# Attention 0 of a two-layer block: smoothing scales loaded ahead of the second half of the context, and tokens rounded in another order of operations

## The reference, cut to what matters

```python
def _div_clamp_fp8(x, scale):
    y = jnp.clip(x.astype(jnp.float32) / scale, -FP8_MAX, FP8_MAX)
    y = y.astype(jnp.bfloat16).astype(jnp.float32)
    return _fp8_roundtrip(y)

def _fp8_linear_pertensor(x, wq, w_scale, in_scale):
    xq = _div_clamp_fp8(x, in_scale)
    return jnp.einsum('bsi,oi->bso', xq * in_scale, wq) * w_scale
...
ln_out = _ln(hidden_states, ln_w, ln_b)
q = _fp8_linear_pertensor(ln_out, wq, wq_scale, q_in_scale).reshape(b, s, g, hpg, d)
...
catq = _div_clamp_fp8(cat, proj_smooth)
return jnp.einsum('bsi,oi->bso', catq, wproj) * (proj_in_scale * proj_w_scale)
```

## Time and profile before

| | before |
|---|---|
| median of 3 runs | 1565.88 us |
| lowest and highest | 1557.8 and 1568.2 us |
| the profiled execution | 1563.18 us, span 1561.4 us |
| PE, PE weight load busy | 88%, 76% |
| DVE busy | 78% |
| ACT, POOL busy | 65%, 50% |

### The profile page before, as it was taken

The page is one execution under the profiler, slowest core; times in us unless marked ns, Lnnn a source line. Parts: engine busy times, 40 slices in busy tenths (PEclk is TensorE's granted clock), DMA queues, the critical chain, the costliest instruction groups (busy, mean ns, idle before and its releaser), DMA issues. The chain is left out here.

```text
span 1561.4 us, 30287 instructions
## 1 busy us (share of the span) xinstructions
PE 1380.8 (88%) x11712; PEld 1183.6 (76%) x11712; DVE 1221.7 (78%) x2380; ACT 1013.3 (65%) x2152; POOL 782.9 (50%) x788
## 2 busy tenths in 40 slices
PE   0577999999999999999999996999779898894995
PEld 0466899999999999999999984677436565563995
DVE  6899888888888888898898897533359887876554
ACT  3687777877878778777777774312147565662773
POOL 4778566566666565666664453101123433331673
PEclk9889999999999999999999998999969998995997
DMA  3100010100100000001010002340350002003563
GB/s 102 47 15 28 15 22 15 32 5 15 35 15 16 22 14 17 20 15 35 15 31 22 1 1 90 70 59 21 66 163 2 14 2 68 1 14 134 186 213 128
DMA packets 62238, 69.84 MB, mean 45 GB/s; under 512 B 5424, under 2 KB 54800, under 8 KB 61968
## 3 DMA queue, kind: packets, MB, share of 16 engines
q1 hardware_dynamic: 59488, 60.54, 13.9%
q0 software_dynamic: 2432, 7.34, 1.4%
q10 hardware_dynamic: 176, 0.04, 0.0%
HBM read 55.56 MB, written 12.34 MB: 43 GB/s over the span
## 5 line engine op out<-in xcount | busy, mean ns | idle before, releaser
L880 POOL TENSOR_TENSOR RB<-YS,M 128x512 bf16<-128x512 f32 x128 | 161.6, 1263 | 245.3 <-DVE YS L740 245.3
L566 ACT ACTIVATE QT<-B,sm 128x256 f32<-128x256 f32 x256 | 130.8, 562 | 163.4 <-PE B L422 163.4
L442 PE MATMUL SS<-QT,KT 128*128 128x256 f32 x512 | 156.8, 401 | 10.0 <-DVE mx L695 10.0
L1748 POOL TENSOR_SCALAR_AFFINE_SELECT P<-P 128x1024 f32<-128x1024 f32 x64 | 82.3, 1285 | 154.3 <-ACT P L1602 154.3
L876 POOL TENSOR_TENSOR yy<-vv,half 128x12 f32<-128x12 f32 x64 | 147.4, 2303 | 5.3
L390 PE MATMUL PA<-WH,XQ 128*128 128x256 f32 x512 | 142.3, 309 | 6.3 <-ACT SQ L595 6.3
L392 PE MATMUL PA<-WL,XQ 128*128 128x256 f32 x512 | 130.5, 286 | 0.0
L714 DVE TENSOR_TENSOR QN<-QN,yy 128x512 f32<-128x512 f32 x128 | 125.0, 977 | 4.1 <-POOL yy L876 4.1
L707 DVE TENSOR_REDUCE vv<-SQ 128x6 f32<-128x768 f32 x128 | 120.6, 942 | 0.4 <-ACT SQ L598 0.4
L695 DVE TENSOR_REDUCE mx<-SS 128x4 bf16<-128x512 f32 x128 | 88.0, 688 | 40.5 <-PE SS L434 39.8
L410 PE MATMUL PA<-W,XB 128*128 128x128 bf16 x1536 | 109.5, 222 | 3.2 <-POOL XB L817 3.2
(11 more groups left out here) (328 smaller groups left out, 4489.8 us busy)
## 6 DMA issues: line engine op xcount, KB each, us to landing
W<-in_w SPq DMA_DIRECT2D x16, 1024.0 KB
Q<-qsc SPq DMA_DIRECT2D x48, 128.0 KB
WR<-in_wprojT SPq DMA_DIRECT2D x16, 256.0 KB, 3.0
K<-ksc SPq DMA_DIRECT2D x12, 256.0 KB
qsc<-T POOLq DMA_DIRECT2D x8, 384.0 KB, 4.2
X<-in_x SPq DMA_DIRECT2D x4, 512.0 KB, 5.7
CR<-in_xctxT SPq DMA_DIRECT2D x8, 256.0 KB, 2.9
RSM<-rsm_d SPq DMA_DIRECT2D x16, 128.0 KB, 4.2
```

What stands on the lines that cost most here:

```text
L442: pe.matmul(SS[:, 256 * z:256 * z + 256], k[:, 128 * z:128 * z + 128], q[:, 256 * z:256 * z + 256], start=True, stop=False)
L566: a.activation(QT[i % 2][:, o:o + 256], B1[:, o:o + 256], ACT.Identity, bias=col(n + "b"), scale=col(n + "w"))
L880: p.tensor_tensor(RB[i % 2][:], YS[:], M[:], ALU.subtract).then_inc(s_rb, 1)
```

## The change

- SP issues the store and the load of the smoothing scales right behind the weights of group 0, and the second half of the context after them.
- ACT scales y by -1/scale (a new tile scn) instead of by 2^20/scale. It no longer signals y by itself, and writes m of chunk i when DVE is done with chunk i-1's place, s_qs i-1, instead of waiting for POOL.
- DVE has two operations for a chunk instead of three: max(m, QMIN) + y into QS, then max(m, QMIN) - QS into QS. Neither y nor m is clamped above. The first of them waits for POOL's chunk i-2.
- POOL clamps QS between -448 and 448 with one tensor_scalar instead of subtracting m.
- DVE has one small operation more at the start, for scn.

```diff
@@ sp_attention_0
-            sp_context(sp, 1)
             sp.wait_ge(s_srv, 1)
             sp.dma_start(rsm_d.rearrange("a (c d) -> (a c) d", d=256), SRR).then_inc(s_sr, 16)
             sp_smooth(sp, 0)
+            sp_context(sp, 1)
@@ act_quad_scale
-            sc = scq[:, k, c:c + 1]
-            a.activation(QY[i % 3][:], LNT[:, c], ACT.Copy, scale=sc).then_inc(s_qy, 1)
+            a.activation(QY[i % 3][:], LNT[:, c], ACT.Copy, scale=scn[:, k, c:c + 1])
             if i >= 2:
-                a.wait_ge(s_q, i - 1)
-            a.activation(QM[i % 2][:], LNT[:, c], ACT.Abs, scale=sc).then_inc(s_qm, 1)
+                a.wait_ge(s_qs, i - 1)
+            a.activation(QM[i % 2][:], LNT[:, c], ACT.Abs, scale=scq[:, k, c:c + 1]).then_inc(s_qm, 1)
@@ dve_quad_round
-            v.wait_ge(s_qy, i + 1)
-            v.tensor_scalar(y[:], y[:], QMAX, -QMAX, ALU.min, ALU.max).then_inc(*vs.up())
             v.wait_ge(s_qm, i + 1)
-            v.tensor_scalar(m[:], m[:], QMIN, QMAX, ALU.max, ALU.min).then_inc(*vs.up())
-            v.wait_ge(*vs.at())
             if i >= 2:
                 v.wait_ge(s_q, i - 1)
-            v.scalar_tensor_tensor(out=s_[:], in0=y[:], scalar=1.0 / TWO20, in1=m[:], op0=ALU.mult, op1=ALU.add).then_inc(s_qs, 1)
+            v.scalar_tensor_tensor(out=s_[:], in0=m[:], scalar=QMIN, in1=y[:], op0=ALU.max, op1=ALU.add).then_inc(*vs.up())
+            v.wait_ge(*vs.at())
+            v.scalar_tensor_tensor(out=s_[:], in0=m[:], scalar=QMIN, in1=s_[:], op0=ALU.max, op1=ALU.subtract).then_inc(s_qs, 1)
@@ pool_quad_round
-            p.tensor_tensor(dst, QS[i % 2][:], QM[i % 2][:], ALU.subtract).then_inc(s_q, 1)
+            p.tensor_scalar(dst, QS[i % 2][:], 448.0, -448.0, ALU.min, ALU.max).then_inc(s_q, 1)
```

More of the change, by code:

```diff
@@ L200, in build @@
         scq = sb("scq", [128, 4, 2])
+        scn = sb("scn", [128, 4, 2])
         csc = sb("csc", [128, 4, 2])
@@ L251, in build @@
         s_zm, s_zroot, s_zv = (sem(n) for n in ("zm", "zroot", "zv"))
-        s_qturn, s_lnt, s_qy, s_qm, s_qs, s_q = (sem(n) for n in ("qturn", "lnt", "qy", "qm", "qs", "q"))
+        s_qturn, s_lnt, s_qm, s_qs, s_q = (sem(n) for n in ("qturn", "lnt", "qm", "qs", "q"))
         s_c, s_ch, s_ctx = (sem(n) for n in ("c", "ch", "ctx"))
@@ L754, in dve_attention_0 @@
             for k in range(4):
-                v.tensor_scalar(scq[:, k, :], scq[:, k, :], TWO20, None, ALU.mult)
-                t = v.tensor_scalar(csc[:, k, :], sm[:, AT[kinds[k]]:AT[kinds[k]] + 2], col(scales[k]), None, ALU.mult)
-            t.then_inc(s_sc, 1)
+                v.tensor_scalar(scn[:, k, :], scq[:, k, :], -1.0, None, ALU.mult).then_inc(*vs.up())
+                v.tensor_scalar(csc[:, k, :], sm[:, AT[kinds[k]]:AT[kinds[k]] + 2], col(scales[k]), None, ALU.mult)
+            v.wait_ge(*vs.at())
+            v.tensor_scalar(scq[:], scq[:], TWO20, None, ALU.mult).then_inc(s_sc, 1)
             v.wait_ge(s_sr, 16)
```

## The result

The changed kernel takes **1553.64 us** (median of 13 runs, 1546.66 to 1558.69) where the kernel before took 1564.48 on the same chip (median of 13, 1557.8 to 1576.11). The ratio is 0.9919, with a 95% interval of 0.9895 to 0.9942: faster by 0.8%. Of the ways that I had set down it is nearest to rival 2, the light clamp (1553 us), to which I had given 14%.

What follows compares the result with a forecast made beforehand. DVE's queue bounds the first 160 us, with a wait for the smoothing scales before the loop. Load -7.5, start +6.7 and loop +11.5 make +10.7 us on the profiled 1563.2, so 1574 us, range 1554 to 1589.

Steps and rivals of the forecast that it cites:

- rival 2: POOL's clamp in each chunk is light, 0.75 us: start -0.9, loop -1.3, together -9.7, 1553 us; chance 0.14.
- The earlier load: Before the loop: smoothing scales stored and loaded sooner, POOL's L838 starts at about 19.5 instead of 26.98, -7.5 us.
- p: Duration of POOL's clamp of 512 columns, L817 in each of 32 chunks, taken as 1.5 us.
- The bound below: Lower bound for POOL's 512-column clamp, from the one-input select L1748: about 0.7 us.
- The mutual exclusion: In the chunks, DVE and POOL shut each other out for whole instructions; whichever asked second waits for all of the other.
- the start: Replay from POOL's L843 to the third group of DVE's L179: +6.7 us with a clamp of 1.5 us.
- the loop: Chunks of quarters 1 to 3, iterations n = 1 to 11, on DVE's path: +11.5 us.
- My formula: Loop cost per iteration: 0.5 + (p - 1.15) for n = 1 to 5, 0.5 + 2 x (p - 1.15) for 6 to 11.
- The term for L732: From n = 6 on, DVE's L732 waits for POOL's second clamp, so p - 1.15 counts twice per iteration.
- the same replay: Start worked through operation by operation on DVE and POOL: +6.7 us with p = 1.5, -0.9 with p = 0.75.
- That ACT's lifted waits give nothing: In the loop, ACT no longer waiting for POOL gains nothing, since DVE was not waiting for ACT.

Runs made afterwards that it cites:

- rounding alone: Changed kernel with the smoothing scales' store and loads back in their old place, so only the new DVE and POOL chunk operations: 1559.34 us, ratio 0.9966 against before.
- the fastest kernel: Changed kernel with DVE's four operations per pair of chunks reordered and POOL's weight scaling L829 as a two-tile tensor_tensor with broadcast scale: 1543.04 us, ratio 0.9852 against before.
- the removed one back: Changed kernel with a third DVE operation per chunk, clamping y in place between -448 and 448 ahead of the other two: 1559.26 us, ratio 0.9942 against before.
- reordered pair: Changed kernel with the adding operations of both chunks of a pair first on DVE, then both subtracting ones: 1547.87 us, ratio 0.9894 against before.
- the series on POOL: Changed kernel with POOL operations of several forms and widths appended behind its last POOL work, in two runs, to price them; kernel time says nothing.
- the first series: Changed kernel with clamp, multiplications and subtraction appended on POOL at 128, 256 and 512 columns; at 512 the clamp took 0.63 us, multiplication by a tile's scale 1.65.

## Why the prediction was wrong

**The earlier load was right**: -7.5 forecast, L838 at 19.38 where I said 19.5, and 7.4 us passed on whole to the last chunk. It landed by the queue as worked out; the store took until 14.17 where I had 13.5.

**The step that failed is p.** The sum took 1.5 us for POOL's clamp of 512 columns, from the line through L829's rows at 128 and 256 columns; it measured 0.61. The bound below was wrong too: 0.7, from the select. I had reasoned that the same instruction in the trace is the nearest row. It was nearest by name; by form (one operation with a scale, against two with constants) it was another price, 1.65 against 0.63. The row of the select, one input and far away by name, gave the value within 0.1. The Trainium skill, "GPSIMD Engine Reference", section "Engine selection", sets GpSimd against VectorE: about twice as slow for operations with two inputs, roughly line rate with one. For the clamp the trace agrees: 0.61 us, no more than DVE's 0.69 for an operation of the same size on two tiles, and the subtraction of two tiles takes 1.04. For a single multiplication or min it does not: 1.50, slower than the subtraction. So neither the rule of the Trainium skill nor my row could be taken alone for every form, and 14% for rival 2 was too little where the two disagreed by a factor of two. That the median came out at rival 2's 1553 us is luck: rival 2 had -9.7 us for load, start and loop together, the traces have -18.1 up to the last chunk, and a part of that doesn't reach the end.

**The mutual exclusion was right, its price too high.** The order of L662, L817 and L664 came as replayed, and the kernels without the clamp (-7.7 us at the last chunk) and with two of them (+12.1) show it on the path. So DVE and POOL do not meet only at semaphores. But I added whole rows: 0.61 + p + 0.05 + 0.61 = 1.88 for the second chunk at p = 0.61, where the rows show 94.72 to 96.34 = 1.62. A row held out shows a little less than the sum of the two, and the same was to be read in the earlier trace rows (L661, asked at 111.03, ends 0.15 after L817 for an operation that alone takes 0.28). The Trainium skill, "SBUF — State Buffer", section "Who interferes with whom", says that the two engines share one pair of ports and lock it exclusively; the trace agrees with it after the change as before, and the exclusion spoke less against the change than I had made of it, since a DVE operation is held up for 0.29 us instead of a microsecond. It does not hold for every row of POOL: in the kernel with two clamps POOL's L878, on 128x12, stands from 95.54 for 2.72 us, and DVE's L662 and L664 on two tiles, at 96.04 and 96.77, kept their 0.70 and 0.69.

This second step would have failed with the right p as well. With two clamps, at 1.3 us for a chunk, my working gives about +4.9 for the start (between its +3.6 at 1.15 and +6.7 at 1.5) and +8.1 for the loop, +13; against before that kernel has +0.4 and +1.0 (35.2 us against 34.8 from L838 to the third group of L179, 92.0 against 91.0 from there to the last chunk). So for start and loop, forecast at +18.2 and measured at -10.5, p accounts for some 16 us by the measured slope (12.1 us for 0.69) and the price of the exclusion for the rest. This is an estimate, since two clamps of 0.61 are not one of 1.3.

**The loop**: +11.5 forecast. From the third group of L179 to the last chunk before took 91.0 us, now 83.6: -7.4. My formula with the measured p gives 5 x (-0.04) + 6 x (-0.58) = -3.7. The other half is in what I had taken for the typical pair. Iteration 7 has 3.26 us, but the last eleven pairs before have 39.6, thus 3.60 each, and after 34.2, thus 3.11 (2.95 in iteration 7). The last pair of before shows why, in the timeline of POOL and then of DVE:

```profile
147.67 1.20 POOL L880 TENSOR_TENSOR RB<-YS,M 128x512 bf16<-128x512 f32 x1
148.83 1.31 POOL L823 TENSOR_TENSOR CL<-CR,CH 128x512 fp32r<-128x512 f32 x1
...
146.61 1.25 DVE L659 TENSOR_SCALAR QY<-QY 128x512 bf16<-128x512 bf16 x1
147.78 1.24 DVE L661 TENSOR_SCALAR QM<-QM 128x512 bf16<-128x512 bf16 x1
149.05 1.64 DVE L665 SCALAR_TENSOR_TENSOR QS<-QY,QM 128x512 f32<-128x512 bf16 x1
```

It took 6.12 us, because each of the first chunk's operations, shown here, met another of POOL's, which iteration 7 doesn't show. The shortest of the eleven pairs take 2.26 us before and 2.65 after, twice the 1.13 and 1.32 of a chunk alone. So a pair took 1.34 us more than that on the mean before and 0.46 after; with two clamps it is 0.89. How much of this is the shorter operation on POOL and how much that DVE has two operations to be met instead of three, the runs don't separate. The term for L732 was right: my formula has 6 x 0.54 = 3.2 for it, and the stretch from L728 to L740, over the first six, fell from 14.3 to 10.9 us. In a group of 22 chunks the costs of before were there to read, from the third group of L179 to the last chunk:

```profile
L665 DVE SCALAR_TENSOR_TENSOR QS<-QY,QM 128x512 f32<-128x512 bf16 x23 | 17.2, 749 | 0.8
L661 DVE TENSOR_SCALAR QM<-QM 128x512 bf16<-128x512 bf16 x22 | 14.8, 673 | 0.0
L659 DVE TENSOR_SCALAR QY<-QY 128x512 bf16<-128x512 bf16 x22 | 11.0, 502 | 0.0
```

Operations that alone take 0.28 had means of 0.67 and 0.50. The same stretch of the changed kernel:

```profile
L664 DVE SCALAR_TENSOR_TENSOR QS<-QM,QS 128x512 f32<-128x512 bf16 x23 | 18.4, 801 | 0.8
L662 DVE SCALAR_TENSOR_TENSOR QS<-QM,QY 128x512 f32<-128x512 bf16 x22 | 17.7, 806 | 1.3 <-ACT QM L535 1.2
```

That is 36.1 us in place of 43.0.

**The start**: +6.7 forecast, -0.9 by the same replay with p = 0.75, -3.1 measured. Two differences show in the rows. The replay let chunk 0 begin at 32.1, when POOL's L843 ends; DVE's L662 in fact began ahead of it, at 23.71, which is 31.3 in the times of before. And of the 3.1 us only 1.45 are won ahead of the thirds, 1.8 behind them, where the load of the output weights and ACT set the time, as I had set down for the light clamp.

**That ACT's lifted waits give nothing** was right within half a microsecond.

**From the end of attention 0 on** I had nothing, and here a part of the gain went. The last L880 is 18.1 us earlier, the end of the profiled execution only 8.3. Two places hold 8.1 of the missing 9.8: the last 24 matmuls of L1077 took 10.63 us instead of 6.03, and the load of Q in the chain that ended last 20.59 instead of 17.14. In the timelines of PE, before and then after:

```profile
1109.03 6.03 PE L1077 MATMUL B<-DW,HD 128*128 128x256 f32 x24 [2.44 <-DVE X L1291]
```

```profile
1091.06 10.63 PE L1077 MATMUL B<-DW,HD 128*128 128x256 f32 x24 [2.43 <-DVE X L1291]
```

By the windows, the stretch from 1070 to 1089 had PE busy 18.63 of 19 us at a granted clock of 1.00, then came the wait of 2.43 us, and from 1091 to 1102 the granted clock was 0.56, near the 1.2 GHz level. Before, PE had been as busy (18.59 of 19) and waited as long, and the clock stayed at 1.00, 2.4 GHz. The records show no difference in what PE did in the 19 us ahead of it. The same 24 matmuls took 9.31 us in the changed kernel's second trace, 10.58 with the load alone, 10.66 with the rounding alone, 10.67 with the clamp twice, 10.65 in the fastest kernel, 9.31 with the clamp left out and with the removed one back, 7.63 in the reordered pair, 7.48 with ACT's old wait, 9.31 and 10.68 in the two with the series on POOL at their end, and 6.03 in both traces of before. So it differs in size from execution to execution of one kernel. Whether it has to do with the change isn't settled: before's two traces are both free of it, and all twelve others have some of it, the kernel that reaches the place at 1105.2 (before is there at 1106.8 and 1109.0) as the one that is there at 1083.2. From the last L880 to the end the two traces of before have 607.4 and 607.8 us, the ten of the table below 608.2 to 618.5.

What that leaves in the medians, all against before (mean of its two traces for the last L880, 952.9; median on the same chip for the time):

| kernel | last L880 earlier by | median lower by |
|---|---|---|
| after | 17.1 | 10.8 |
| after, again | 15.8 | 15.0 |
| load alone | 6.8 | 10.5 |
| rounding alone | 9.4 | 5.7 |
| clamp twice | 4.1 | 2.3 |
| ACT's old wait | 16.5 | 17.1 |
| clamp left out | 23.7 | 21.5 |
| removed clamp back | 7.0 | 8.3 |
| reordered pair | 19.0 | 15.9 |
| the same with L829 | 23.7 | 24.2 |

The second column is 14.3 on the mean, the third 13.1. What is won in attention 0 comes out at the end but for a microsecond or so, with a scatter of several; the 8.3 of one pair of profiles and the 10.8 of the first comparison stand at the low end of it.

So the sum as it should have been: -7.5 for the load, -3.1 for the start, -7.4 for the loop, some -18 at the end of the stretch, of which 11 to 15 are seen in the medians.

## What to carry to other kernels

The nearest row is the one that has the same form, not the same name: before a price is drawn from another operation of an instruction, hold the number of operations and the kind of operands against it, and where a far row with the right number of inputs says half as much, give the two the same weight. Where two engines shut each other out, take the cost of a moved operation from the mean of its whole group, as it stands in the loop, and not from one iteration that looks clean. An operation that is light on POOL but stands between two of DVE's is worth what it holds, 0.24 us here. Issuing DVE's independent operations together got back 1.5 of these 7.7 us.

## What the runs showed of the hardware that I had not expected

- A TENSOR_SCALAR on POOL of 128x512 f32 takes 1.50 us with one operation, 0.62 to 0.68 with the pairs min and max, multiply and multiply, multiply and add, and 1.93 with add and add or min and multiply. Adding a multiplication by 1 to a scale from a tile brings it from 1.65 (in the first series) to 0.70.
- A multiplication by a broadcast column takes 1.06 us on POOL as an operation on two tiles and 1.65 as one with a scale; at 128 columns 0.40 and 0.67.
- A clamp on POOL whose row shows 0.61 us holds up a DVE operation on two tiles by 0.29; an operation of POOL on 128x12 whose row shows 2.72 us left such operations at 0.69 and 0.70.
- The granted clock of one and the same stretch behind one and the same wait was 1.00 in two executions and 0.56 in another with no difference in the records of what PE did in the 19 us ahead of it.
